# Layer 3 of a four-layer network: ScalarE rounds the next weight chunk at the end of the odd slots instead of in the even slots

## The reference, cut to what matters

```python
def _L3_cond_ref(x, router_logits, skill_gate, skill_up, skill_down, shared_gate, shared_up, shared_down):
    ...
    # two chosen experts of 8 per batch, and one shared expert; each is
    return jnp.einsum('bsi,ih->bsh', jax.nn.gelu(g, approximate=True) * u, down_w)   # g = x@gate, u = x@up, i = 1024

def _L3_ffn_ref(x, gamma1, Wq, bq, Wdown, bdown, Wup, bup, Wo, bo, gamma2, Wg, bg, We):
    h = _rmsnorm(x, gamma1)
    q = (h @ Wq + bq).reshape(b, t, H, HD)
    kv = ((h @ Wdown + bdown) @ Wup + bup).reshape(b, t, H, 2 * HD)
    att = jnp.einsum('bthd,btgd->bthg', q, k) / np.sqrt(HD).astype(np.float32)
    att = jax.nn.softmax(att, axis=-1)
    out = jnp.einsum('bthg,btgd->bthd', att, v).reshape(b, t, D)
    x = x + (out @ Wo + bo)
    ...
    combined = jnp.einsum('btd,edf,bte->btf', h2, We, gate)
    return x + combined
```

## Time and profile before

| what | before |
|---|---|
| median of 3 runs | 1621.95 us (1607.72 to 1625.82) |
| the profiled execution | 1616.93 us |
| its span, first to last instruction | 1615.1 us |
| mean granted TensorE clock | 0.887 |
| PE / DVE / POOL / ACT busy | 82% / 66% / 43% / 35% |

### The profile page before, as it was taken

How to read it: one execution, slowest core, us unless ns; L and a number is a source line. 1 busy time by engine, 2 the same in 40 slices (tenths; PEclk the granted TensorE clock), 3 DMA queues, 4 the chain that set the end, 5 groups by cost and what they waited for, 6 DMA issues and landing times.

```text
span 1615.1 us, 18388 instructions
## 1 busy us (share of the span) xinstructions
PE 1324.5 (82%) x6484; PEld 1115.6 (69%) x6484; DVE 1068.1 (66%) x1880; ACT 564.9 (35%) x883; POOL 689.3 (43%) x318
## 2 busy tenths in 40 slices
PE   4998897998894799548889999977988888967528
PEld 3897785897782699537677887766777667755317
DVE  7598666498663555536765333788479946995984
ACT  2302212302210588505445445434533444322001
POOL 3320113720005467563003534667456844763652
PEclk9899797899796899869999999999999999977858
DMA  5400001400006699831001322121212221200001
GB/s 170 143 27 14 14 30 41 152 27 1 0 10 219 203 291 313 257 108 40 0 1 59 124 98 79 59 79 59 85 40 85 91 72 52 66 14 26 26 26 39
DMA packets 51947, 130.83 MB, mean 81 GB/s; under 512 B 6400, under 2 KB 29968, under 8 KB 51728
## 3 DMA queue, kind: packets, MB, share of 16 engines
q1 hardware_dynamic: 44016, 111.96, 21.5%
q0 software_dynamic: 4608, 12.59, 2.4%
q10 hardware_dynamic: 3232, 5.11, 0.9%
HBM read 107.35 MB, written 22.28 MB: 80 GB/s over the span
## 4 chain that ended last, share of the span: by engine, by line
PE 40%; DVE 17%; issue 9%; POOL 6%; ACT 4%; another core or an unknown queue 2%; DMA 1%; ACTq 1%; SPq 0%; DVEq 0%; POOLq 0%
PE bank L375 13%; PE bank L378 12%; PE bank L379 12%; DVE G L397 3%; POOL VW L397 3%; DVE acc L2001 2%; POOL w_lo L567 2%; DVE bank L1977 2%; DVE F L2001 1%; ACT w_hi L1327 1%; PE bank L828 1%; PE bank L998 1%; DVE acc L2133 1%; DVE xT L1914 1%
## 5 line engine op out<-in xcount | busy, mean ns | idle before, releaser
L567 POOL TENSOR_TENSOR w_lo<-raw,w_hi 128x1536 fp32r<-128x1536 f32 x48 | 169.6, 3533 | 249.4 <-ACT w_hi L1327 234.1
L375 PE MATMUL bank<-x_hi,w_hi 128*128 128x512 f32 (+1 forms) x560 | 221.1, 395 | 54.2 <-POOL w_lo L567 25.6
L378 PE MATMUL bank<-x_lo,w_hi 128*128 128x512 f32 (+1 forms) x560 | 214.8, 384 | 0.0
L379 PE MATMUL bank<-x_hi,w_lo 128*128 128x512 f32 (+1 forms) x560 | 214.4, 383 | 0.0
L375 PEld LDWEIGHTS bank<-x_hi,w_hi 128*128 128x128 f32 x560 | 111.1, 198 | 83.5 <-POOL w_lo L567 32.5
L375 PE MATMUL bank<-hid_hi,w_hi 128*128 128x512 f32 x328 | 134.6, 410 | 31.9 <-DVE hid_lo L1932 15.6
L378 PE MATMUL bank<-hid_lo,w_hi 128*128 128x512 f32 x328 | 132.0, 403 | 0.0
L379 PE MATMUL bank<-hid_hi,w_lo 128*128 128x512 f32 x328 | 131.5, 401 | 0.0
L1430 ACT ACTIVATE hid_hi<-bank 128x512 fp32r<-128x512 f32 x96 | 57.5, 599 | 195.4 <-DVE bank L1977 195.4
L379 PEld LDWEIGHTS bank<-x_hi,w_lo 128*128 128x128 f32 x560 | 111.1, 198 | 19.8
L378 PEld LDWEIGHTS bank<-x_lo,w_hi 128*128 128x128 f32 x560 | 111.2, 199 | 17.9
(11 more groups left out here) (407 smaller groups left out, 3587.5 us busy)
## 6 DMA issues: line engine op xcount, KB each, us to landing
raw<-in_skill SPq DMA_DIRECT2D x32, 768.0 KB
raw<-in_shared SPq DMA_DIRECT2D x16, 768.0 KB
raw<-in_l1e SPq DMA_DIRECT2D x20, 513.0 KB
base<-xs SPq DMA_DIRECT2D x38, 256.0 KB, 4.5
ys<-F SPq DMA_DIRECT2D x38, 256.0 KB, 4.9
VW<-in_l1e SPq DMA_DIRECT2D x18, 513.0 KB, 5.0
K<-in_l3e SPq DMA_DIRECT2D x16, 512.0 KB
raw<-in_l0c SPq DMA_DIRECT2D x12, 512.0 KB
```

Of the source, the lines that this page charges most:

```text
L375: i = nc.tensor.matmul(out, sh, mh, start=first, stop=False)
L378: nc.tensor.matmul(out, sh, ml, start=False, stop=False)
L379: return nc.tensor.matmul(out, sl, mh, start=False, stop=last)
L567: nc.gpsimd.tensor_tensor(w_lo[n % W3_SLOTS][:], raw[n % 2][:], w_hi[n % W3_SLOTS][:].bitcast(F32), ALU.subtract).then_inc(w_ready.sem, 1)
```

## The change

`dense_hi(n)` for the chunks 13 to 47 leaves its place in the even slot 2n - 2, behind that slot's `hid_hi`, and goes to the end of the odd slot 2n - 3, behind all that ACT does there (of the attention, of the finish, and of a special chunk). The first of them, chunk 13, is now rounded at the end of 0.23. The chunks 2 to 12 stay where they are. ACT's instructions are as many as before, and the lists of PE, DVE, POOL and SP are the same. Lines behind the first edit move up by one: L1424 and L1430 are L1423 and L1429 in the changed kernel.

```diff
@@ -1412,8 +1412,7 @@
-                    next_chunk = i % 2 == 0 and 2 <= n < CHUNKS3 * BATCH
-                    if next_chunk and b == 0:
+                    if b == 0 and i % 2 == 0 and n >= 2:
                         dense_hi(n)
                     if b < BATCH:
...
@@ -1428,14 +1427,15 @@
                         nc.scalar.activation(hid_hi[0][:, g % HID3, :], PB[g % 2][1][:], ACT.Copy).then_inc(g3_hi.sem, 1)
-                    if next_chunk and b > 0:
-                        dense_hi(n)
                     if 0 <= q < BATCH:
                         attention3_after(q, i)
                     if 0 <= p < BATCH:
                         finish3_after(p, i)
                     if special_at(b, i) is not None:
                         special_hi(special_at(b, i))
+                    n = CHUNKS3 * b + (i + 1) // 2 + 1
+                    if i % 2 == 1 and CHUNKS3 < n < CHUNKS3 * BATCH:
+                        dense_hi(n)
                     if i == 5 and 1 <= b < BATCH - 1:
                         nc.scalar.activation(x_hi[(b + 1) % 2][:], xT[b + 1][:], ACT.Copy).then_inc(x3_hi.sem, 1)
```

## The result

| what | before | changed |
|---|---|---|
| median, 13 runs each on one chip | 1613.73 us (1605.5 to 1627.97) | 1628.81 us (1623.93 to 1636.7) |
| the profiled execution | 1616.93 us | 1633.67 us |
| its span | 1615.1 us | 1631.9 us |
| mean granted TensorE clock | 0.887 | 0.876 |

The ratio of the changed kernel to the one before is 1.0099, with a 95% interval of 1.0069 to 1.0129: the change costs 1% or 15 us. The two profiled executions differ by 16.8 us of span.

A forecast was written before the change was run, and what follows sets the result against it. DVE, with blocks by POOL, was taken to set the pace of the attention's pairs. The terms -2.4 + 14.2 - 6.0 + 3.1 = +8.9 us on the profiled 1616.93 us gave 1626 us, range 1602 to 1636.

The forecast's parts named there:

- the meetings: Attention slots where DVE's and POOL's two-input operations ask for the shared port together: POOL first by about 0.1 us, chance 0.45.
- the pairs: Pairs of attention slots with a chunk and two products, in loops 1 to 3: 13.3 us against 11.2, together 14.2 lost.
- a rounding ahead of something awaited: Slots 1.20, 2.12 and 3.12: the rounding delays gelu, and in 1.20 the residue meets a product; loss 3.1 us.
- Its other signs: Prediction wrong if a POOL wait for `w_hi` stays; if right, the product group's mean in 1.12 to 1.17 is near 3.1 us.
- Slots 1.0 to 1.11: Start of loop 1, no products yet and PE the bound: its waits for the residue go, gain 2.4 us.
- The walk: One attention pair timed from an odd slot's product: POOL ahead by about 0.1 us, the pair 13.3 us against 11.2.
- the gelu of slot 2.3: DVE's wait there for ACT goes, as the norm's root no longer stands behind a rounding: 1.2 us off the pairs' loss.
- The softmax: Slot 18 of loops 1 to 3: DVE's subtraction no longer stands still for the residue; 2.0 us each, gain 6.0 us.
- the part on slots 2.4 to 2.21: Slots 2.4 to 2.21 and 3.4 to 3.21: last experts load DVE and PE; nothing counted beyond the other terms.
- PE's waits: Rival: PE's waits for the residue come back whole, -25.1 us, giving 1592 us; chance 0.08.
- Blocks in loops 2 and 3: Rival: nine more pairs, in scores and values of loops 2 and 3, lose 2.1 us each, giving 1645 us; chance 0.10.

The follow-up runs named there:

- Experiments 4 and 5: Changed kernel, ACT's list kept: POOL's residue waits for DVE at slots 20 and 12 (ratio 1.0058), or every moved residue waits for its old `hid_hi` (0.9989).
- experiment 8: Changed kernel, but POOL's product of every half sweep waits for DVE's and the roundings of slots 19 and 11 are late again: ratios 0.9848 and 0.9907.
- experiment 3: Changed kernel, but the five roundings of slots 19 and 11 are back at their old place: 1592.96 us, ratio 1.0011 to the kernel before.
- experiment 6: Changed kernel, but the five roundings are late again and POOL's even product waits for DVE's: 1601.26 us, ratio 0.9946 to the kernel before.
- experiment 5: Changed kernel with ACT's list kept, but each moved residue of POOL waits for the `hid_hi` of its old place: 1608.47 us, ratio 0.9989.
- experiments 1 and 7: Changed kernel, but POOL's even product waits for DVE's (1586.05 us, ratio 0.9973), or computes one of its four groups only (1610.17 us, one profiled run).

## Why the prediction was right, and where its terms were off

The forecast was 1626 us from 1617, +8.9 us; the measured medians are 1628.8 from 1613.7, +15 us, and the loops' own difference is +19.9. The direction held, and so did the mechanism where the forecast had walked it: POOL wins the meetings, and DVE stands still behind it. That the number came out within 3 us of the forecast is in good part luck: the pairs were forecast 8 us too high, the term for a rounding ahead of something awaited 19 us too low, and the two errors have opposite signs. The measured terms are -2.6 + 5.8 - 7.3 + 21.9 = 17.8, and 2.2 us more lie in the stretches 2.3 to 2.10, 3.3 to 3.10 and 3.21 to 3.23, to which the sum gave nothing.

The place was wrong too. The sum put 5.7 us of its 8.9 into loop 1 and 1.7 and 1.5 into loops 2 and 3; measured are 1.8, 10.2 and 7.8. The prediction had named a change of more than 3 us in each of them as a sign that it is wrong, and that sign appeared. Its other signs hold in part: in the pairs POOL's wait for the rounding is down to 0.26 us, but 142.9 us of such waits stay in all, and the six score products of loop 1 have a mean of 2.9 us, not 3.1.

Term by term:

- **Slots 1.0 to 1.11, -2.4:** measured -2.6, in every kernel with the early rounding. Right.
- **The meetings.** The walk gave POOL the port by about 0.1 us and 13.3 us a pair; measured 0.09 us and 13.30. The Trainium skill's warning on the ends of POOL's spans (Perfetto Trace Analysis, "GPSIMD Engine Instruction") had left the meeting open by half the margin; here the trace doesn't bear it out as a danger, since the starts and the reported ends agreed within 0.03 us (1033.73 + 4.19 against 1037.89). The even products measured 3.37 and the odd 3.06. The forecast says 3.4 and 2.9; its own walk (asked at 10.26, ended at 13.3) gives 3.0 for the odd.
- **The pairs, +14.2:** the mechanism right, the size too large, and this is the first of the two terms that were off. The changed kernel shows 3.8 (1.11 to 1.17) + 1.6 (1.21 to 2.3) + 0.4 (2.21 to 3.3) = 5.8 us. Two reasons show. In 1.12 DVE was there first (1.39 us, asked 0.27 us ahead of POOL's product at 1026.90), so loop 1's scores have two pairs of the walk, not three. And 1.21 to 2.3 began late after slot 20; with slot 19's rounding put back it shows +7.1, and the three stretches 3.7 + 7.1 + 1.3 = 12.1 us. The sum took each term as if the others weren't there. The 1.2 us that it took off for the gelu of slot 2.3 came back as 0.7 (DVE's wait there is 0.49 us).
- **The softmax, -6.0:** measured 1.23 us for L2019 in all three loops, and -2.0 - 2.7 - 2.7 = -7.3 us. Right, a little low.
- **Where the rounding stands ahead of something awaited, +3.1:** this step failed, in size and in kind. Measured +4.7, +4.4 and +4.4 at slots 19 to 21, +5.0 and +3.4 at slots 10 to 13, 21.9 us. I costed a late gelu, and that part was right where I could see it: 0.60 us of DVE's wait in 2.12. What I didn't cost is that the residue, let go by this rounding, meets the next two-input operation of DVE, whichever that is. In slot 20 it is the normalising step L2026, which pays 4.17 - 1.22 = 2.95 us, in each loop; in slot 12 it is the small products L2080 and L2081, which pay 0.43 us to the residue and 2.08 to POOL's product right behind it. I had walked the products alone, saw the meeting in 1.20 only, for 1.0 us, and counted nothing in loops 2 and 3, as the part on slots 2.4 to 2.21 said. Experiments 4 and 5, which leave ACT's order and hold the residue back, show that it is mostly this: L2026 and L2081 are back at 1.22 and 0.19 us, and PE's idle time in 2.12 is 4.7 to 4.8 us in place of 7.3, 0.7 above the kernel before. The blocks account for 3 x 2.95 + 2 x 2.5 = 13.9 of the 21.9 us and the late gelu of slots 12 for 1.2; the rest I can't divide, and much of it goes with the clock.
- **PE's clock.** It had no term. The time at half clock in loops 1 to 3 went from 34 to 79 us, and PE's busy time rose by 13.4 us of the 19.9. What such time costs alone is seen in stretches that differ from another execution in the clock and neither in DVE's busy time nor in PE's idle time by more than 0.2 us: 3.4 us more at half clock took 1.6 us (experiment 8, one kernel twice), and 10.3 us more took 3.9 (2.10 to 2.13 in experiment 3, 3.10 to 3.13 in experiment 6). That it is a consequence of POOL's times and no cause of its own is suggested by experiment 5, which holds only POOL back and has 44 us of it, against 79. But no run changed the clock alone, and its exact part of the 19.9 us stays open.

The rivals: PE's waits did come back nearly whole (25.1 to 3.6 us) and were worth 2.6 us, because what stood behind them was DVE. Blocks in loops 2 and 3 came, though at slots 12 and 20 rather than in the pairs that this rival named, and with them nearly the whole of the loss; that rival had a chance of 0.10. The difference of the loops alone, +19.9 us on the profiled 1616.93, would be 1636.8, just over the range's end of 1636; the medians differ by less.

The Trainium skill's rule that the order of issue decides who stands still (SBUF — State Buffer, "Who interferes with whom") agrees with experiments 1 and 7: 0.1 us of order is 2.1 us of a pair (13.30 against 11.15), and DVE's duration follows POOL's one for one.

## What to carry to other kernels

Before moving a producer earlier, list every operation of the other engine that can stand still behind what this lets go (here DVE's two-input operations behind POOL's), small ones too, and ask at each which of the two comes first. Where two engines meet within a tenth of a microsecond, settle the order with a wait in favour of the engine that is the bound. Here that line alone was worth little or nothing (ratio 0.9966, with 1 inside the interval) and the move alone cost 1%, but the line and the move of 30 of the 35 roundings together gave 0.985 to 0.991. Terms worked out one by one don't add where one shifts the other's phase: here 5.8 us appeared in place of 12.1.
